# A gated cross-attention block on one core: which engine issues the second phase's DMAs

## The reference

```
x1  = x + tanh(g_xattn) * (y + softmax(q k^T + bias, masked) v Wo^T)
out = x1 + tanh(g_ffn) * (z base_W^T + base_b + sum_e w_e (z A_e^T) B_e^T * 2),   z = layernorm(x1)
```

## Time and profile before

| | us |
|---|---|
| median of three runs | 879.33 |
| lowest, highest | 877.48, 880.64 |
| profiled execution | 884.5 |
| its span | 882.3 |

### The profile page before, as it was taken

The page is one execution under the profiler, slowest core; times in us unless marked ns, Lnnn a source line. Parts: engine busy times, 40 slices in busy tenths (PEclk is TensorE's granted clock), DMA queues, the critical chain, the costliest instruction groups (busy, mean ns, idle before and its releaser), DMA issues.

```text
span 882.3 us, 13927 instructions
## 1 busy us (share of the span) xinstructions
PE 847.7 (96%) x4212; PEld 712.1 (81%) x4212; DVE 699.9 (79%) x1172; ACT 494.7 (56%) x1185; POOL 496.1 (56%) x352
## 2 busy tenths in 40 slices
PE   7999999999999998889999999999999999987898
PEld 5887888778888887778888888888888888876786
DVE  6888777877766666568888889889988989899664
ACT  6566776666676753456555555555555555546210
POOL 0353534653465532557576776777667666757422
PEclk9999999999999999899999999999999999999799
DMA  8876677579777785987988888898898898884001
GB/s 291 309 280 246 249 276 274 215 294 360 275 299 274 274 309 156 284 270 227 259 230 264 241 249 255 249 259 252 250 257 246 251 260 253 273 262 140 25 25 72
DMA packets 155392, 214.72 MB, mean 243 GB/s; under 512 B 10960, under 2 KB 109392, under 8 KB 154960
## 3 DMA queue, kind: packets, MB, share of 16 engines
q1 hardware_dynamic: 155344, 214.13, 75.6%
HBM read 128.11 MB, written 85.98 MB: 243 GB/s over the span
## 4 chain that ended last, share of the span: by engine, by line
PE 32%; DMA 24%; DVE 24%; ACT 7%; issue 5%; SPq 4%; POOL 1%; DVEq 0%; ACTq 0%; POOLq 0%
DMA pT<-p_rows 11%; DMA p_rows<-p_blocks 10%; DVE p_norm L1128 6%; PE Sb L1417 4%; PE Sb L1418 4%; PE Sb L1419 4%; ACT p_exp L773 4%; SPq L346 4%; DVE unit_out L950 2%; PE Ab L1417 2%; PE Ab L1418 2%; PE Ab L1419 2%; DVE p_blocks L1134 2%; DVE rscale L1123 2%; DMA v_raw<-wv 2%
## 5 line engine op out<-in xcount | busy, mean ns | idle before, releaser
L495 POOL TENSOR_TENSOR w_lo<-w_raw,w_hi 128x1280 fp32r<-128x1280 f32 (+1 forms) x29 | 84.8, 2924 | 122.7 <-ACT w_hi L639 122.7
L544 POOL TENSOR_TENSOR P_hl<-pT,P_hl 128x512 fp32r<-128x512 f32 x64 | 82.8, 1294 | 103.1 <-ACT P_hl L639 103.1
L539 POOL TENSOR_TENSOR a_rest<-small_a,A_hi 128x512 f32<-128x512 f32 x64 | 89.9, 1404 | 47.3 <-ACT small_a L767 47.1
L639 ACT ACTIVATE P_hl<-pT 128x512 fp32r<-128x512 f32 x64 | 40.5, 633 | 124.7 <-DMA pT<-p_rows 124.7
L773 ACT ACTIVATE p_exp<-s_sb,negmax 128x128 f32<-128x128 f32 x256 | 99.0, 389 | 10.2 <-DVE negmax L1105 9.7
L532 POOL TENSOR_TENSOR bm<-bias,maskneg 128x512 f32<-128x512 f32 x64 | 84.1, 1313 | 17.7 <-DVE s_sb L1111 11.9
L1128 DVE TENSOR_TENSOR p_norm<-p_exp,rscale 128x512 f32<-128x512 f32 x64 | 90.2, 1410 | 2.3
L1588 PE MATMUL Ab<-P_hl,V_hi 128*128 128x256 f32 x256 | 65.8, 335 | 17.6 <-POOL P_hl L544 14.4
L639 ACT ACTIVATE A_hi<-Ab 128x512 fp32r<-128x512 f32 x64 | 38.3, 598 | 67.9 <-PE Ab L1589 67.9
L639 ACT ACTIVATE U<-Sb 128x512 f32<-128x512 f32 x90 | 53.6, 600 | 40.5 <-PE Sb L1419 39.9
L639 ACT ACTIVATE w_hi<-w_raw 128x512 fp32r<-128x512 f32 (+2 forms) x67 | 60.2, 903 | 22.5 <-PE Kb L1419 6.7
(11 more groups left out here) (300 smaller groups left out, 2703.2 us busy)
## 6 DMA issues: line engine op xcount, KB each, us to landing
qk_units<-unit_out SPq DMA_DIRECT2D x128, 512.0 KB, 3.3
qk<-qk_units SPq DMA_DIRECT2D x64, 1024.0 KB, 7.3
p_rows<-p_blocks SPq DMA_DIRECT2D x64, 256.0 KB, 2.7
pT<-p_rows SPq DMA_DIRECT2D x256, 64.0 KB, 4.2
w_raw<-wqk SPq DMA_DIRECT2D x31, 512.0 KB, 4.3
v_raw<-wv SPq DMA_DIRECT2D x32, 256.0 KB, 4.8
o_raw<-wo SPq DMA_DIRECT2D x32, 256.0 KB, 4.7
stage<-ctxT SPq DMA_DIRECT2D x8, 256.0 KB, 5.7
```

What stands on the lines that cost most here:

```text
L495: pool.tensor_tensor(w_lo[:, n % 2, first:5, :], w_raw[:, n % 2, first:5, :], f32(w_hi[:, n % 2, first:5, :]), ALU.subtract).then_inc(w1_l ...
L539: pool.tensor_tensor(a_rest[:, :, :], small_a[:, :, :], f32(A_hi[:, r, :, :]), ALU.subtract).then_inc(a_rest_done, 1)
L544: pool.tensor_tensor(blocked(P_hl[:, :, 1, :]), queries(pT[:, r, :, :, :]), f32(blocked(P_hl[:, :, 0, :])), ALU.subtract).then_inc(p_lo_do ...
L639: act.activation(dst, src, ACT.Copy).then_inc(done, 1)
```

## The change

SP keeps, in the second phase, the exchange of P's blocks, the last unit stores, x again and the output. ScalarE's program gets, with their waits:

- the loads of units 2 and 3 before and after the exponentials of unit 0, those of units 4 and 5 and the first two chunks of Wv of group 1 ahead of P_hl of units 0 and 1;
- in each step, between `V_hi` and `P_hl`: a wait for the scores of unit t, the load of unit t + 2, the chunk of Wv or Wo, and once per group the bias; at unit 7 the wait for the landing of the last unit stores;
- in the last group, loraR and lora_B at b = 2 (SP had them at b = 0) and baseT at b = 4 (SP had it at b = 3).

The splits of loraR, lora_B and baseT on ScalarE and POOL come one unit later (b = 4, 5, 6 and 7 instead of 3, 4, 5, 6 and 7); two chunks of baseT instead of one are split behind the loop. The helpers `load_wv`, `load_wo`, `load_bias` and `load_unit` take the issuing engine as an argument and are otherwise the same. In the first units a wait of SP on `m_done[4]` falls away.

```diff
 # SP
-            def first_units():
-                for i in range(4):
-                    sp.wait_ge(st[i], 16 * (G + 2))
-                sp.wait_ge(scores_done, 1)
-                load_unit(0, 2)
-                store_blocks(0, 0)
-                load_blocks(0, 0)
...
+            for b in range(3):
+                store_blocks(0, b)
+                load_blocks(0, b)
 
             def group(g, q):
...
                 for b in range(4 if first else 0, B):
-                    if first and b == 7:
-                        for i in range(4):
-                            sp.wait_ge(st[i], 16 * JOBS)
                     before = (g, b - 1) if b > 0 else (g - 1, B - 1)
                     store_blocks(*before)
-                    if not (last and b >= B - 2):
-                        sp.wait_ge(scores_done, B * g + b + 1)
-                        load_unit(g + (b + 2) // B, (b + 2) % B)
                     load_blocks(*before)
-                    if 2 <= b <= 5 and not last:
-                        load_wv(g + 1, 1 - q, b - 2)
...
-                    if first and b > 3 and b < 7:
+                    if first and b < 7:
                         store((R22, R21, R12)[b - 4], JOBS - 1)
 # ScalarE, step(g, b, q)
                 v_evict_hi(t, b)
+                if first and b == 7:
+                    for i in range(4):
+                        act.wait_ge(st[i], 16 * JOBS)
+                if not (last and b >= B - 2):
+                    act.wait_ge(scores_done, t + 1)
+                    load_unit(act, g + (b + 2) // B, (b + 2) % B)
+                if 2 <= b <= 5 and not last:
+                    load_wv(act, g + 1, 1 - q, b - 2)
+                if b >= 6 and not last:
+                    load_wo(act, g + 1, 1 - q, b - 6)
+                if b < 2 and not first:
+                    load_wo(act, g, q, b + 2)
+                if b == (4 if first else 1) and not last:
+                    load_bias(act, g + 1, 1 - q)
+                if last and b == 2:
+                    act.wait_ge(v_done, LAST)
+                    act.dma_start(loraR_raw, loraR).then_inc(ld_lora, 16)
+                    act.dma_start(loraB_raw, lora_B).then_inc(ld_loraB, 16)
+                if last and b == 4:
+                    act.wait_ge(o_done, LAST)
+                    act.dma_start(base_raw[:, :, :], baseT).then_inc(ld_base, 16)
                 probs_hi(t - 2, b % 2, B // 2 * g + b // 2)
 # ScalarE, end of the first phase
                 if n == JOBS - 1:
+                    for i in range(4):
+                        act.wait_ge(st[i], 16 * (G + 4))
+                    act.wait_ge(scores_done, 1)
+                    load_unit(act, 0, 2)
                     exponentials(0)
+                    act.wait_ge(scores_done, 2)
+                    load_unit(act, 0, 3)
...
+            act.wait_ge(scores_done, 3)
+            load_unit(act, 0, 4)
+            load_wv(act, 1, 1, 0)
             probs_hi(0, 0, 1)
...
+            act.wait_ge(scores_done, 4)
+            load_unit(act, 0, 5)
+            load_wv(act, 1, 1, 1)
             probs_hi(1, 1, 1)
```

More of the change, by code:

```diff
@@ L308, in build, with load_wv, load_wo, load_bias @@
         out_ring = [flat(p_exp), out_more[:, :]]
+        def load_wv(eng, g, q, k):
+            if k == 0:
+                reached(eng, v_done, B * (g - 1))
+            eng.dma_start(v_raw[q][:, k, :], wv[g, :, k, :]).then_inc(ld_wv[k], 16)
+        def load_wo(eng, g, q, k):
+            if k == 0:
+                reached(eng, o_done, B * (g - 1))
+            eng.dma_start(o_raw[q][:, k, :], wo[g, :, k, :]).then_inc(ld_o[k], 16)
+        def load_bias(eng, g, q):
+            reached(eng, bm_done, B * (g - 1))
+            eng.dma_start(bias4[:, q, :, :], bias[g, :, :, :]).then_inc(ld_bias, 16)
+        def load_unit(eng, g, b):
+            eng.dma_start(f32(qk[:, b % 2, :, :, :]).rearrange("p h a k -> p (h a) k"),
+                         qk_units[2 * g + b // BH, :, :, b % BH, :]).then_inc(ld_qk[b % 2], 16)
         @block.sync
@@ L451, in group @@
                             sp.dma_start(x_again[:, j, :], x[:, j, :]).then_inc(ld_x2[j], 16)
-                        sp.wait_ge(v_done, LAST)
-                        sp.dma_start(loraR_raw, loraR).then_inc(ld_lora, 16)
-                        sp.dma_start(loraB_raw, lora_B).then_inc(ld_loraB, 16)
                     if last and b >= 2:
@@ L457, in group @@
                         sp.dma_start(x_again[:, b % 2, :], x[:, b, :]).then_inc(ld_x2[b % 2], 16)
-                    if last and b == 3:
-                        sp.wait_ge(o_done, LAST)
-                        sp.dma_start(base_raw[:, :, :], baseT).then_inc(ld_base, 16)
-            first_units()
             group(0, 0)
@@ L618, in _ @@
             late_root(3)
-            late_low(5, w_base_lo[:, 3, :], base_raw[:, 3, :], w_base_hi[:, 3, :])
+            for k in (2, 3):
+                late_low(2 + k, w_base_lo[:, k, :], base_raw[:, k, :], w_base_hi[:, k, :])
             a_remainder(UNITS - 2, 0)
@@ L807, in step @@
                     split_wo_hi(g + 1, 1 - q, 0)
-                if last and b == 3:
+                if last and b == 4:
                     act.wait_ge(ld_lora, 16)
                     late_high(loraR_hi, loraR_raw)
-                if last and b == 4:
+                if last and b == 5:
                     act.wait_ge(ld_loraB, 16)
@@ L814, in step @@
                 exponentials(t)
-                if last and b >= 5:
+                if last and b >= 6:
                     act.wait_ge(ld_base, 16)
-                    late_high(w_base_hi[:, b - 5, :], base_raw[:, b - 5, :])
+                    late_high(w_base_hi[:, b - 6, :], base_raw[:, b - 6, :])
             plain_first_hi(0)
@@ L927, in _ @@
             y_hi(0)
-            late_high(w_base_hi[:, 3, :], base_raw[:, 3, :])
+            for k in (2, 3):
+                late_high(w_base_hi[:, k, :], base_raw[:, k, :])
             probs_hi(UNITS - 2, 0, UNITS // 2)
```

48 lines of the change are left out of this document (7 added, 41 removed).

## The result

The changed kernel takes 974.91 us (median of four runs, 966.61 to 977.62) where the kernel before takes 879.27 (four runs, 877.48 to 880.64): ratio 1.1077, 95% interval 1.1011 to 1.1143. The forecast was 866. The profiled execution took 977.6, with a span of 975.4 at a mean granted clock of 0.944.

The account below looks back on a forecast made before the run. TensorE was taken as the bound in the steady stretch, with 16.2 us lost in the start. Terms 13.9 - 2.5 - 1.0 - 0.3 + 2.0 + 1.0 = 13.1 us off the median 879.33 gave 866, range 857 to 879.

Parts of the forecast that it names:

- the one on the landing: Start of second phase: unit 2's store of P's blocks lands in 2.6 us, the steady median; other bound 5.3.
- the fourth part: Steady stretch: P's loads come some 1 us sooner behind an earlier unit load; gain 2.0 us, bounds 0 and 5.4.
- signs of being wrong: Landing above 4.8 us in steady stretch with TensorE waiting on P_hl; 5.3 still in start; ScalarE waiting several us at unit 7.
- the rival of no change: Start: traffic matters, not order in one queue; only SP's issues leave its chain, 2.5 us, 876.8; chance 0.08.
- The slower rival: Every steady step: unit load issued ahead of the store; 888 at a 5.3 us landing, 923 at 7.26; chance 0.12.
- 17.2 + L: Steady stretch: a unit's chain to the third unit's scores, L the store's landing, against TensorE's 22.0 us; decides from L = 4.8.
- The start: Units 2 to 10: 16.2 us lost; with loads off SP, unit 10 starts at 392.0 instead of 405.88, 13.9 us gained.
- 7.91 us wait for v_raw: Start: ScalarE stood until 355.80 for a Wv chunk SP issued late; its disappearance was a sign of being right.
- sign of being right: Start: stores of P's blocks landing in under 4 us, beside unit 10's scores starting at 392 to 396.
- The wait for the last unit stores: Unit 7: SP's 4.3 us wait becomes ScalarE's; 2.5 us taken off, bounds 0 and 4.3.
- ScalarE's issues: Each step: 1.0 us per unit, 1.4 with bias, hidden by its pT wait; 0.3 us taken off for issues ahead of the phase.
- The last group: End of kernel: two of SP's four loads move to ScalarE, later; gain 1.0 us, bounds -1.5 and 2.7.

Follow-up runs that it names:

- e1: The changed kernel plus a ScalarE wait so the unit load is issued with SP's store of P's blocks, not before; 917.14 us, ratio 1.0357.
- e2: The kernel before, all on SP's one queue, with the unit load ahead of the store of P's blocks in each step; 1072.5 us, ratio 1.2109.
- e8: The changed kernel with chunk, bias and unit load all behind the exponentials on ScalarE, no wait added; 972.81 us, ratio 1.1041.
- e5: e1 with the chunks and the bias moved behind the exponentials on ScalarE; 891.81 us, ratio 1.0087.
- e6: The changed kernel with the chunks and the bias moved behind the exponentials on ScalarE, unit load left in place; 932.8 us, ratio 1.0551.
- y3: y1 with the wait for the last unit stores moved to ahead of group 2 and the last group's first four loads spread; 873.88 us, ratio 0.9867.
- e4: The kernel before plus ScalarE's new wait for the scores, all DMAs staying on SP; 884.58 us, ratio 0.9992.
- e3: The changed kernel with unit loads from step 4 on back on SP behind the store, chunks and bias staying on ScalarE; 887.1 us, ratio 1.0028.
- y1: The kernel before with only the first units reordered: loads of units 3 and 4 right behind a store; 877.33 us, ratio 0.9936.
- y4: y3 with the unit load from step 4 on behind P's four loads instead of between store and loads; 1047.99 us, ratio 1.1903.

## Why the prediction was wrong

**The step that failed** is the one on the landing: "store at 340.5, landed at 343.1 (2.6 us, the steady median ...)" for a store no longer behind a load on its own queue, and with it the fourth part, that in the steady stretch P's loads "come some 1 us sooner". Both took a queue for a path of its own. The prediction had the right row (7.26 us from a store behind a load) and a rival built on it, and let "the two shared one queue" decide against it. The runs show 7.02 us with the load on another queue (packets: none of the store's in 3 us), 2.4 with the same two queues and the store first (e1), 7.6 with one queue and the load first (e2). The order in time is the cause; the queue is none. Of its signs of being wrong the landing above 4.8 us came true in 25 of the 53 steps, with TensorE waiting on `P_hl`, and the median of all 53, 4.4 us, would have hidden it.

**The rules on queues.** The Trainium skill ("DMA: Bandwidth & Descriptors", Issuing engines are not separate DMA queues) was right in what matters here: the landings followed the traffic of all issuers. The prediction made of it the rival of no change, by reading "only SP's issues leave its chain"; it overlooked that a new issuer also moves the load ahead of the store. By what the Trainium skill states on the same page under Queues, rings and completion order (each engine takes turns between the queues that it has work for), read as the prediction read it, a store beside a load should get packets in turn with it. The packets show no turns: issued beside the load it moved ahead of it (191 packets to 4), issued 1.01 us later it got none for 3 us. Whether the engines had the store's packets and left them, or had not been given them yet, the trace doesn't tell.

**The slower rival was the right mechanism, mis-sized.** It had 17.2 + L for three steps, so 24.2 us at L = 7.02, and 923 us in all at 7.26, with every step alike. From the scores at 598.87 to those at 627.52, through the late store at 608.46, three steps took 28.65 us, 4.4 more. Two terms are missing. P's loads count with 1.75 + 2.8 = 4.55 us in the sum; here ScalarE starts on them 8.25 us after their first issue (615.48 to 623.73), 3.7 us more. Of these, 1.6 were in the prediction's own rows: 2.8 us is the start's landing, and a steady step has 4.4. With it the sum is 18.8 + L, and the deciding point 3.2 us and not 4.8; e8 is 10% slower with a median landing of 4.1, its P's loads late as well. For the other 2.1 us, the next unit load and chunk (614.77, 615.43) went ahead of P's loads. And the application runs at 1.2 GHz, 1.77 us (625.75 to 627.52) instead of 0.9: 0.9 us. e1 prices the store's share by itself: 7.2 of the 10.8 points in ratio. The other 3.6 are shared by P's loads and what follows from them; e5 removes another 2.7, e6 shows that the two don't add up singly (e1 and the chunk's move alone give 7.2 and 5.3 back, together 9.9).

**The start** was counted rightly in its loss, wrongly in its remedy. Most of the 16.2 us lost come from unit loads ahead of stores: y3, which for the start only turns that order round and moves one wait, takes 63.3 us to unit 10 instead of 74.8 and has it at 395.05, inside the forecast's own 392 to 396. The change itself reached it only here, 19 us past the end of that range:

```profile
415.32 0.52 PE L1562 MATMUL Sb<-qk 128*128 128x256 f32 x1
```

The 7.91 us wait for v_raw is gone as foreseen. But the order went wrong in both ways. P's first loads were issued at 331.66 to 334.70 with ScalarE's unit load and chunk (332.91, 333.50) in their midst, and P was usable at 341.27, after a wait of 7.90 us of ScalarE and one of 3.10 us of TensorE behind it; and the store 1.24 us behind the chunk (334.74) took 6.94 us. The eight stores up to unit 10 land in 6.6 us in the median, where under 4 was the sign of being right. The wait for the last unit stores, priced at 2.5 us, held ScalarE some 1.3 (its V_hi ends at 387.25, the load that follows is issued at 388.56).

**ScalarE's issues** cost about what was taken from SP's rows: 0.57 us for a unit, a median of 0.58 to 0.62 for a chunk (0.43 was taken), and the time was hidden but for one step: 16 times P was there before ScalarE had issued its loads, and one of these (351.09) has a wait of TensorE behind it, 0.66 us. Its new wait on the scores cost nothing (e4), and e3 with chunks and bias on ScalarE is no slower than before. That the clock follows the waits held too, in the other direction.

**The last group** can't be told apart in after, where P is late there too; y3 against y1, 0.7% in ratio, bundles the spreading of its loads with the moved wait, and their intervals touch, so neither part's gain is shown by itself.

**Left open:** why a second queue doesn't pass. The packets show the order and not its cause. That the end of the issue decides fits all 40 stores of after and e6 that came less than 0.75 us behind a unit load, but no run was made to test it. Nor was it tried whether smaller pieces of the unit load would let the store in.

## What to carry to other kernels

Before a DMA is moved to another engine, write down for each latency-critical transfer what is issued in the microseconds ahead of it (5 here, with loads of 1024 KB), from any engine: moving an issue earlier puts it ahead of others, and a second queue gives no way past. Put bulk loads right behind the first leg of a round trip, so that they move while its landing is awaited and the second leg is issued. And where an engine's program holds one such round trip per step, add up its own round (landing and issues) as a bound of its own: e2 and y4 ran at it, and in y4, as in the old start, being late is what kept the loads ahead of the next store.

## What the runs showed of the hardware

- A 256 KB store on one queue issued 1.01 us behind a 1024 KB and a 256 KB load on another moved no packet between 1.0 and 4.0 us after its issue, although these loads moved only 0.74 MB in that time (245 GB/s, where the start of the kernel has 284); it landed in 7.02 us. Issued 0.09 us behind the load, it landed in 2.85 and moved ahead of it (191 packets to 4 from 600.8 to 601.7 us).
- Of two issues on two queues the one that ended first went first. 40 stores of after and e6 were issued less than 0.75 us behind a unit load: 29 whose issue (0.34 us) ended before the load's (0.57 us) landed in 2.3 to 3.4 us, 11 whose issue ended behind it in 4.2 to 6.8.
- The same 4 x 64 KB loads land in 1.9 us with nothing ahead of them (e2, y4), in 4.4 behind a unit load issued 2 us ahead of them, of which a median of 11% has moved, in 5.6 with the load issued into their midst (e8).
- TensorE's clock is lower behind its waits: 61.9 us more of idleness between units 10 and 63 came with 26.2 us more of busy time for the same matmuls, 0.4 us for each us of waiting.
